# Row order instead of column pairs: the layout of the two middle products in a log-polar convolution kernel

## The chip, the cores and the metric

The kernel runs on one core of a Trainium2 chip. The metric is the device time of one execution in microseconds (us): 1636.28 us is the median of three runs before the change (1635.61 to 1636.46). Five engines work side by side and meet at semaphores: TensorE (PE in the profile) multiplies, VectorE (DVE) and ScalarE (ACT) prepare its inputs and take its results, GpSimd (POOL) and SyncE (SP) start transfers.

## The reference, cut to what matters

```python
def log_pooling(x):                      # x: 32 images, 256 channels, 28 x 28
    y = conv(x per channel, MASKS, pad 4)        # 12 fixed masks of 9 x 9, each an average of a bin
    ...                                          # laid out as 4 x 3 values for each pixel
xp = log_pooling(x)
out = conv(xp, w_conv1, stride (4, 3))           # 256 -> 256 channels, 12 values per pixel
out = out + conv(x, w_center, 1 x 1) + b_center
mean, var = over images and pixels, per channel
out = (out - mean) * rsqrt(var + EPS) * gamma + beta
return relu(out + x)
```

So each pixel gets 12 neighbourhood averages and itself, and a product with a 256 x 256 matrix for each. The six averages of the inner ring (next neighbours) are small sums of single pixels, the six of the outer ring are sums of larger boxes.

## The kernel before, in words

An image lies with its width W = 28 as the outer and its height H = 28 as the inner dimension: "column" u is a run of 28 values. A channel half (c = 0, 1; 128 partitions) of an image is one step s = 2 * image + c. The 256 output channels are two halves o = 0, 1. All inputs of TensorE are split into a high and a low part of fp32, and each product is three matmuls (hi*hi, lo weight*hi input, hi weight*lo input: the function `products`, lines 670 to 672).

The work on a pair of neighbouring image columns is shared: with U = 14 pairs, D1 = even + odd column and D2 = odd - even column are 14 columns of 28 = 392 values (HALF). Their products M1 and M2 (taps TAP_M1 and TAP_M2, three vertical shifts each) go into PSUM banks 4 to 7; the sum and the difference of M1 and M2 give the two columns of a pair of the output. This is "the middle": the inner-ring and centre taps that stand in one column.

In the kernel before, D1, D2, M1 and M2 are stored in STRIPES = 7 stripes of STRIPE = 56 values. A stripe holds two columns interleaved: value (h, k) with k the column in the stripe stands at 2 * h + k. A tap that is shifted by one row is therefore shifted by 2 values within every stripe, and covers SHORTER = 54 of its 56 values: a matmul over 7 runs of 54 with a pitch of 56.

For each image VectorE (one in-order queue) works through, for c = 0 and then c = 1:

1. four instructions that make the inner inputs: the differences `d03`, then D1, then D2 (392 values each, written in stripes), then the vertical sums VD (`v_ready`);
2. for c = 0, `take_middle` of the image before: M2 from PSUM and M1 from its copy `m1_copy` are added and subtracted into `y_stage`, one half o at a time;
3. when ScalarE has made the high parts (`split_inner`, line 370; it waits for `v_ready` and for `inner_done`, which TensorE sends after the inner products of the step before), the low part of the inner inputs;
4. the box sums, their pooled pairs and low parts (j = 0, 1, 2); for c = 0, behind the low part of j = 0, `take_y` of the image before, which adds banks 0 to 3 to `y_stage` and sends `y_ready`.

For each step TensorE (in order) does 36 matmuls of the middle, 24 of 392 columns for the other inner taps (behind `y_ready` for c = 0, since they start banks 0 to 3 anew), and 72 of 364 columns for the outer ring. After the last image a second phase loads y and x of all images again, scales, adds and stores them; it is bound by its transfers.

Of the kernel before, what the change touches and what calls it, by code (L numbers as in the profile page):

```python
# [7 lines left out]
def conv_bn_relu_program(nc, x, x_wide, w_raw, b_center, gamma, beta, out, y_dram):  # L8
# [7 lines left out]
    IMAGES, P, CH, W, H = x.shape  # L16
# [4 lines left out]
    HW = H * W  # L21
    U = W // 2
    HALF = U * H
# [4 lines left out]

    STRIPES, STRIPE = U // 2, 2 * H
    SHORTER = STRIPE - 2
    TALL = H + 2


# [27 lines left out]
    BANK = 512  # L64
    MBANK = 2 * CH

    ctx = ExitStack()
    with ctx:
# [6 lines left out]
        def view(buf, first, *dims):  # L75
            whole = buf[:, :]
            return bass.AP(whole.tensor, whole.offset + first, [list(whole.ap[0]), *map(list, dims)])

        start_of, end_of, used = {}, {}, [0]
        with ExitStack() as phase1:  # L80
# [16 lines left out]
            inner = reused("inner", 4 * HALF)  # L97
            pooled = reused("pooled", 2 * PAIR)
            INNER = 6 * HALF
            inner_split = reused("inner_split", 2 * INNER, F32R)  # L100
# [5 lines left out]
        y_stage = sb("y_stage", CH * HW)  # L106
        m1_copy = sb("m1_copy", CH * HALF)

        D1, D2, VD, SD = 0, HALF, 2 * HALF, 4 * HALF
# [55 lines left out]
        acc = ctx.enter_context(nc.psum_tensor("acc", [P, 8 * BANK], F32))  # L165
# [30 lines left out]
        middle_taken = sem("middle_taken")  # L196
# [250 lines left out]
        def _(dve):  # L447
            add = lambda out_, a, b: nc.vector.tensor_tensor(out_, a, b, ALU.add)  # L448
            sub = lambda out_, a, b: nc.vector.tensor_tensor(out_, a, b, ALU.subtract)  # L449
# [43 lines left out]
                        in1=view(hi, hi_at, (1, (b - a) * CHANNELS)).bitcast(F32),  # L493
                        op0=ALU.mult, op1=ALU.subtract).then_inc(w_lo_ready, 1)

            striped = (STRIPE, STRIPES), (1, 2), (2, H)
            every_other_column = (4 * H, STRIPES), (2 * H, 2), (1, H)

            def take_middle(image):

                dve.wait_ge(m1_copied, image + 1)
                wait_from_one(dve, y_saved, 16 * image)
                wait_from_one(dve, y_measured, MOMENTS * image)
                for o in range(CH):
                    m2 = view(acc, (MBANK + CH + o) * BANK, *striped)
                    m1 = view(m1_copy, o * HALF, *striped)
                    add(view(y_stage, o * HW, *every_other_column), m2, m1)
                    last = sub(view(y_stage, o * HW + H, *every_other_column), m1, m2)
                last.then_inc(middle_taken, 1)

            def take_y(image):
                dve.wait_ge(pooled_done, PAIRS * CH * (image + 1))
# [41 lines left out]
            def image_steps(image, first=False, second=False):  # L554
                for c in range(CH):
                    s = CH * image + c

                    def columns(first_column, step, n, *more):
                        return view(x_pad, c * X_PAD + (first_column + 2) * H, *more, (step * H, n), (1, H))

                    dve.wait_ge(x_loaded[c], 16 * (image + 1))
                    wait_from_one(dve, inner_lo_ready, 2 * s)
                    sub(view(d03, 1, (U * TALL, 2), (TALL, U), (1, H)),
                        columns(-1, 2, U, (H, 2)), columns(1, 2, U, (H, 2))).then_inc(d_ready, 1)
                    even, odd = (view(x_pad, c * X_PAD + (q + 2) * H, *every_other_column) for q in range(2))
                    add(view(inner, D1, *striped), even, odd)
                    sub(view(inner, D2, *striped), odd, even)
                    dve.wait_ge(d_ready, s + 1)
                    add(view(inner, VD, (HALF, 2), (H, U), (1, H)),
                        view(d03, 0, (U * TALL + 1, 2), (TALL, U), (1, H)),  # L570
                        view(d03, 1, (U * TALL + 1, 2), (TALL, U), (1, H))).then_inc(v_ready, 1)
                    if first:
                        lo_of_weights(c, range(INNER_GROUPS))
                    if c == 0 and not first:
                        take_middle(image - 1)

                    dve.wait_ge(inner_hi_ready, 2 * s + 1)
                    sub(view(inner_split, INNER, (1, SD)), view(inner, 0, (1, SD)),
                        view(inner_split, 0, (1, SD)).bitcast(F32)).then_inc(inner_lo_ready, 1)

                    dve.wait_ge(row2_ready, 16 * (s + 1))
                    add(view(row3, 1, (ROW3_H, W + 2), (1, H)), view(row2, 4, (ROW2_H, W + 2), (1, H)),
                        columns(0, 1, W + 2)).then_inc(row3_ready, 1)

                    dve.wait_ge(row3_ready, s + 1)
                    add(view(row3v, 2, (ROW3V_H, W + 2), (1, H + 1)), view(row3, 0, (ROW3_H, W + 2), (1, H + 1)),
                        view(row3, 1, (ROW3_H, W + 2), (1, H + 1))).then_inc(row3v_ready, 1)

                    dve.wait_ge(inner_hi_ready, 2 * s + 2)
                    sub(view(inner_split, INNER + SD, (HALF, 2), (H, U), (1, H)),  # L590
                        view(d03, 2, (U * TALL - 2, 2), (TALL, U), (1, H)),
                        view(inner_split, SD, (HALF, 2), (H, U), (1, H)).bitcast(F32)).then_inc(inner_lo_ready, 1)

                    if first:
                        lo_of_weights(c, range(FIRST_OUTER_GROUP - 1, len(GROUPS)))
                        if c == 0:
                            transform_weights(1)

                    dve.wait_ge(row3v_ready, s + 1)
                    add(view(box4, 0, (BOX4_H, W + 2), (1, H + 3)), view(row3v, 0, (ROW3V_H, W + 2), (1, H + 3)),  # L600
                        view(row3v, 2, (ROW3V_H, W + 2), (1, H + 3))).then_inc(box4_ready, 1)
                    add(view(box3, 1, (BOX3_H, W + 2), (1, H + 2)), view(row3v, 1, (ROW3V_H, W + 2), (1, H + 2)),
                        view(row3, 1, (ROW3_H, W + 2), (1, H + 2))).then_inc(box3_ready, 1)

                    dve.wait_ge(box4_ready, s + 1)
                    pooled_sums(s, c, 0, box4, 0, 4 * BOX4_H + 3, BOX4_H, row2, 0, 5 * ROW2_H + 8, ROW2_H)
                    dve.wait_ge(box3_ready, s + 1)
                    pooled_sums(s, c, 1, box3, 4, 4 * BOX3_H - 4, BOX3_H, row2, 8, 5 * ROW2_H - 8, ROW2_H)
                    lo_of_pooled(s, c, 0)
                    if c == 0 and not first:  # L610
                        take_y(image - 1)
                    dve.wait_ge(ends_ready, 16 * (s + 1))
                    short_sum(s, c, 0)
                    short_sum(s, c, 1).then_inc(pooled_ready, 1)
                    lo_of_pooled(s, c, 1)
                    lo_of_pooled(s, c, 2)
                    if second and c == 0:
                        make_pivot()
# [44 lines left out]
        def _(pe):  # L663
            def products(c, o, tap, place, buf, hi, lo, *dims, start=False, stop=False):

                hi_w, hi_at = w_part(c, 0, tap)
                lo_w, lo_at = w_part(c, 1, tap)
                hi_w, lo_w = (view(w, at + o * P, (1, P)) for w, at in ((hi_w, hi_at), (lo_w, lo_at)))
                hi_in, lo_in = view(buf, hi, *dims), view(buf, lo, *dims)
                nc.tensor.matmul(place, hi_w, hi_in, start=start, stop=False)  # L670
                nc.tensor.matmul(place, lo_w, hi_in, start=False, stop=False)  # L671
                return nc.tensor.matmul(place, hi_w, lo_in, start=False, stop=stop)  # L672
# [8 lines left out]
            with pe.Fori(0, IMAGES) as image:  # L681
                for c in range(CH):
# [5 lines left out]
                    for m, (tap, data) in enumerate(((TAP_M1, D1), (TAP_M2, D2))):  # L688
                        for o in range(CH):
                            bank = (MBANK + CH * m + o) * BANK  # L690
                            products(c, o, tap + 1, view(acc, bank, (1, HALF)),
                                     inner_split, data, INNER + data, (1, HALF), start=c == 0)

                            shorter = (STRIPE, STRIPES), (1, SHORTER)
                            products(c, o, tap, view(acc, bank + 2, *shorter),
                                     inner_split, data, INNER + data, *shorter)
                            last = products(c, o, tap + 2, view(acc, bank, *shorter),
                                            inner_split, data + 2, INNER + data + 2, *shorter, stop=c == CH - 1)
                    if c == CH - 1:
                        last.then_inc(m_done, 1)  # L700
                    pe.wait_ge(w_lo_ready, c * len(GROUPS) + INNER_GROUPS)
# [1 line left out]
                    for o in range(CH):  # L703
                        if c == 0:
                            pe.wait_ge(y_ready, CH * image + FREE)
                        for q, (with_v, with_d) in enumerate(((TAP_D, TAP_C), (TAP_A, TAP_F))):
# [4 lines left out]
                            last = products(c, o, with_d, place, inner_split, at, INNER + at, (1, HALF))  # L711
# [58 lines left out]
```

## Time and profile before

| what | value |
|---|---|
| median of three runs | 1636.28 us |
| the profiled execution's own time | 1636.42 us |
| its span, first to last instruction | 1634.7 us |
| PE busy | 1460.9 us (89%), 8468 matmuls |
| DVE busy | 1421.3 us (87%), 1391 instructions |
| ACT busy | 640.0 us (39%) |
| second phase (scale, add, store) | from about 1480 us on, with TensorE done |

Busy time is the union of an engine's instructions. A matmul's record overlaps the next one's, so its cost in a stream is read from the distance between starts, not from its duration. VectorE's records overlap by about 0.09 us in the same way. The granted clock is that of TensorE: 1.00 is 2.4 GHz, 0.50 is 1.2 GHz. "Idle before, releaser" is the time an engine stood still ahead of an instruction and what ended it.

### The profile page before, as it was taken

To read this page: it belongs to the slowest core of one execution; us is meant where nothing else is said; L and a number is where in the kernel's file an instruction comes from. 1 tells how busy PE (TensorE), PEld (TensorE's weight loads), DVE (VectorE), ACT (ScalarE), POOL (GpSimd) and SP (SyncE) were. 2 spreads that over 40 slices of the span, in tenths; PEclk is the share of its full clock that TensorE was granted. 3 is DMA by queue.
4 is the path that set the end of the run, shared out by engine and by line. 5 is a ranking of instruction groups with operands and counts; after the bars stand their busy time and mean duration, and the time that the engine had idled before them with its cause. 6 is when DMAs were issued, how large, how long until landed. Compare 5 with 4: busy or idle time off the path is not lost.

```text
span 1634.7 us, 22849 instructions
## 1 busy us (share of the span) xinstructions
PE 1460.9 (89%) x8468; PEld 1459.7 (89%) x8468; DVE 1421.3 (87%) x1391; ACT 640.0 (39%) x689; POOL 112.3 (7%) x144
## 2 busy tenths in 40 slices
PE   6999999999999999999999999999999999992000
PEld 6899999999999999999999999999999999992000
DVE  7999999999999999999999999999999999986323
ACT  3334434434334343433433334433343334335423
POOL 1000000000000000000000000000000000000000
PEclk8999999999999999999999999999999999996555
DMA  6455554555555555455554555545555555579999
GB/s 200 108 132 146 136 134 127 125 144 128 120 123 134 142 136 139 127 127 136 136 121 118 139 132 138 144 125 128 132 141 128 112 133 132 136 271 420 425 425 379
DMA packets 65479, 268.75 MB, mean 164 GB/s; under 512 B 7616, under 2 KB 7616, under 8 KB 65472
## 3 DMA queue, kind: packets, MB, share of 16 engines
q1 hardware_dynamic: 42176, 173.38, 31.4%
q0 software_dynamic: 18432, 69.61, 24.6%
q10 hardware_dynamic: 4864, 25.69, 3.8%
q8 instruction: 2, 0.03, 0.0%
q14 instruction: 5, 0.04, 0.0%
HBM read 218.07 MB, written 50.58 MB: 164 GB/s over the span
## 4 chain that ended last, share of the span: by engine, by line
PE 86%; SPq 5%; DMA 4%; DVE 3%; ACT 1%; issue 1%; ACTq 0%; DVEq 0%; POOLq 0%
PE acc L671 29%; PE acc L672 29%; PE acc L670 28%; SPq L311 4%; DMA phase<-x 2%; SPq L308 2%; DMA row<-x_wide 1%; DMA out<-phase 1%; DVE pooled L448 1%; DVE pooled_split L449 0%; ACT phase L440 0%; DVE inner_split L449 0%; ACT m_copy L396 0%; DVE y_stage L448 0%; DVE row3v L448 0%
## 5 line engine op out<-in xcount | busy, mean ns | idle before, releaser
L380 ACT ACTIVATE pooled_split<-pooled 128x1456 fp32r<-128x1456 f32 x192 | 273.5, 1425 | 609.5 <-DVE pooled L448 609.5
L449 DVE TENSOR_TENSOR pooled_split<-pooled,pooled_split 128x1456 fp32r<-128x1456 f32 x192 | 314.9, 1667 | 0.3 <-ACT pooled_split L380 0.3
L670 PE MATMUL acc<-pooled_split,w_first 128*128 128x364 f32 x768 | 252.7, 329 | 4.8 <-DVE pooled_split L449 4.8
L671 PE MATMUL acc<-pooled_split,w_first 128*128 128x364 f32 x768 | 253.6, 330 | 0.0
L672 PE MATMUL acc<-pooled_split,w_first 128*128 128x364 f32 x768 | 253.5, 330 | 0.0
L672 PE MATMUL acc<-pooled_split,w_outer 128*128 128x364 f32 x768 | 252.8, 329 | 0.0
L671 PE MATMUL acc<-pooled_split,w_outer 128*128 128x364 f32 x768 | 252.5, 329 | 0.0
L670 PE MATMUL acc<-pooled_split,w_outer 128*128 128x364 f32 x768 | 252.0, 328 | 0.0
L670 PE MATMUL acc<-inner_split,w_first 128*128 128x392 f32 (+1 forms) x640 | 219.5, 343 | 13.0 <-DVE inner_split L449 9.0
L672 PE MATMUL acc<-inner_split,w_first 128*128 128x392 f32 (+1 forms) x640 | 218.3, 341 | 0.0
L671 PE MATMUL acc<-inner_split,w_first 128*128 128x392 f32 (+1 forms) x640 | 218.1, 341 | 0.0
L671 PE MATMUL acc<-inner_split,w_inner 128*128 128x392 f32 (+1 forms) x640 | 218.0, 341 | 0.0
L672 PE MATMUL acc<-inner_split,w_inner 128*128 128x392 f32 (+1 forms) x640 | 217.5, 340 | 0.0
L670 PE MATMUL acc<-inner_split,w_inner 128*128 128x392 f32 (+1 forms) x640 | 217.2, 339 | 0.0
L448 DVE TENSOR_TENSOR pooled<-box,row 128x1456 f32<-128x1456 f32 x128 | 208.2, 1668 | 0.0
L449 DVE TENSOR_TENSOR inner_split<-inner,inner_split 128x1568 fp32r<-128x1568 f32 x64 | 114.6, 1791 | 95.7 <-ACT inner_split L370 95.7
L370 ACT ACTIVATE inner_split<-inner 128x1568 fp32r<-128x1568 f32 x64 | 96.9, 1514 | 188.7 <-PE acc L672 167.8
L670 PEld LDWEIGHTS acc<-pooled_split,w_first 128*128 128x128 f32 x768 | 145.0, 189 | 5.1 <-DVE pooled_split L449 5.1
L672 PEld LDWEIGHTS acc<-pooled_split,w_first 128*128 128x128 f32 x768 | 144.8, 189 | 0.0
L671 PEld LDWEIGHTS acc<-pooled_split,w_first 128*128 128x128 f32 x768 | 144.7, 188 | 0.0
L671 PEld LDWEIGHTS acc<-pooled_split,w_outer 128*128 128x128 f32 x768 | 144.5, 188 | 0.0
L672 PEld LDWEIGHTS acc<-pooled_split,w_outer 128*128 128x128 f32 x768 | 144.4, 188 | 0.0
(80 smaller groups left out, 2146.6 us busy)
## 6 DMA issues: line engine op xcount, KB each, us to landing
row<-x_wide SPq DMA_DIRECT2D x64, 558.0 KB, 3.7
row<-x_wide POOLq DMA_DIRECT2D x64, 558.0 KB, 7.3
ends<-x_wide SPq DMA_DIRECT2D x64, 504.0 KB, 3.9
ends<-x_wide POOLq DMA_DIRECT2D x64, 504.0 KB, 5.9
x_pad<-x SPq DMA_DIRECT2D x64, 392.0 KB, 3.1
y_dram<-y_stage SPq DMA_DIRECT2D x31, 784.0 KB, 8.5
phase<-y_dram SPq DMA_DIRECT2D x30, 784.0 KB, 29.2
phase<-x SPq DMA_DIRECT2D x30, 784.0 KB, 30.2
```

The costliest lines, as they stand in the source:

```text
L308: sp.dma_start(y_slot(d), y_dram[tail_image(round_, d)]).then_inc(tail_loaded[d], 16)
L311: sp.dma_start(x_slot_whole(d), x[tail_image(round_, d)].rearrange("p c w h -> p c (w h)"))\
L370: nc.scalar.activation(view(inner_split, 0, (1, SD)), view(inner, 0, (1, SD)), ACT.Copy)\
L380: nc.scalar.activation(view(pooled_split, 2 * j * PAIR, (1, PAIR)), view(pooled, (PAIRS * c + j) % 2 * PAIR, (1, PAIR)), ACT.Copy)\
L448: add = lambda out_, a, b: nc.vector.tensor_tensor(out_, a, b, ALU.add)
L449: sub = lambda out_, a, b: nc.vector.tensor_tensor(out_, a, b, ALU.subtract)
L670: nc.tensor.matmul(place, hi_w, hi_in, start=start, stop=False)
L671: nc.tensor.matmul(place, lo_w, hi_in, start=False, stop=False)
L672: return nc.tensor.matmul(place, hi_w, lo_in, start=False, stop=stop)
```

## The change

The interleaved stripes are replaced by whole rows: value (h, u) of D1, D2, M1 and M2 stands at 14 * h + u. A shift by one row is then a shift by 14 values in one run of 378 (HALF - U). On VectorE the two instructions that write D1 and D2 write neighbouring values 14 words (56 bytes) apart instead of 2 words (8 bytes), and `take_middle` reads M1 and M2 at that step. As both halves o now fit one access pattern, `take_middle` has two instructions of 784 values instead of four of 392.

```diff
-    STRIPES, STRIPE = U // 2, 2 * H
-    SHORTER = STRIPE - 2
+    SHORTER = HALF - U
...
-            striped = (STRIPE, STRIPES), (1, 2), (2, H)
-            every_other_column = (4 * H, STRIPES), (2 * H, 2), (1, H)
+            by_rows = (1, U), (U, H)
+            every_other_column = (2 * H, U), (1, H)
...
-                for o in range(CH):
-                    m2 = view(acc, (MBANK + CH + o) * BANK, *striped)
-                    m1 = view(m1_copy, o * HALF, *striped)
-                    add(view(y_stage, o * HW, *every_other_column), m2, m1)
-                    last = sub(view(y_stage, o * HW + H, *every_other_column), m1, m2)
-                last.then_inc(middle_taken, 1)
+                m2 = view(acc, (MBANK + CH) * BANK, (BANK, CH), *by_rows)
+                m1 = view(m1_copy, 0, (HALF, CH), *by_rows)
+                add(view(y_stage, 0, (HW, CH), *every_other_column), m2, m1)
+                sub(view(y_stage, H, (HW, CH), *every_other_column), m1, m2).then_inc(middle_taken, 1)
...
-                    add(view(inner, D1, *striped), even, odd)
-                    sub(view(inner, D2, *striped), odd, even)
+                    add(view(inner, D1, *by_rows), even, odd)
+                    sub(view(inner, D2, *by_rows), odd, even)
...
-                            shorter = (STRIPE, STRIPES), (1, SHORTER)
-                            products(c, o, tap, view(acc, bank + 2, *shorter),
-                                     inner_split, data, INNER + data, *shorter)
-                            last = products(c, o, tap + 2, view(acc, bank, *shorter),
-                                            inner_split, data + 2, INNER + data + 2, *shorter, stop=c == CH - 1)
+                            products(c, o, tap, view(acc, bank + U, (1, SHORTER)),
+                                     inner_split, data, INNER + data, (1, SHORTER))
+                            last = products(c, o, tap + 2, view(acc, bank, (1, SHORTER)),
+                                            inner_split, data + U, INNER + data + U, (1, SHORTER), stop=c == CH - 1)
```

VectorE's queue in the loop over images, c = 0, from the differences `d` to the low part of the inner inputs, before the change:

```order
L449 TENSOR_TENSOR d<-x_pad 128x28x28
L448 TENSOR_TENSOR inner<-x_pad 128x7x2x28
L449 TENSOR_TENSOR inner<-x_pad 128x7x2x28
L568 REGISTER_ALU
L448 TENSOR_TENSOR inner<-d 128x784
L220 ISA
L220 REGISTER_ALU
L448 TENSOR_TENSOR y_stage<-acc,m_copy 128x14x28
L449 TENSOR_TENSOR y_stage<-m_copy,acc 128x14x28
L448 TENSOR_TENSOR y_stage<-acc,m_copy 128x14x28
L449 TENSOR_TENSOR y_stage<-m_copy,acc 128x14x28
```

and in the same place after it:

```order
L447 TENSOR_TENSOR d<-x_pad 128x28x28
L446 TENSOR_TENSOR inner<-x_pad 128x14x28
L447 TENSOR_TENSOR inner<-x_pad 128x14x28
L564 REGISTER_ALU
L446 TENSOR_TENSOR inner<-d 128x784
L218 ISA
L218 REGISTER_ALU
L446 TENSOR_TENSOR y_stage<-acc,m_copy 128x28x28
L447 TENSOR_TENSOR y_stage<-m_copy,acc 128x28x28
```

Nothing is moved: the four instructions of `take_middle` become two of twice the size, and D1 and D2 (`inner<-x_pad`) keep their place. TensorE's queue keeps its 132 matmuls for each step in the same order; 24 of the 36 of the middle read 378 values in one run instead of 7 times 54.

## Rows read from the trace of the kernel before

**Rows 1.** Busy time by stretch (--windows): PE, PEld, DVE, ACT, POOL, clock, DMA share, GB/s.
```profile
100.00:1440.00 1340.00, 1340.00 (x7816) 1340.00 (x7815) 1242.48 (x1190) 528.13 (x560) 102.95 (x119) 1.00 0.54 131
1460.00:1500.00 40.00, 20.18 (x119) 19.88 (x117) 21.50 (x38) 14.86 (x21) 0.00 (x0) 0.78 1.01 419
1500.00:1634.00 134.00, 0.00 (x0) 0.00 (x0) 50.84 (x53) 50.79 (x55) 0.00 (x0) 0.50 0.99 413
```
**Rows 2.** VectorE's timeline, one image in the loop: start, us, instruction, idle before.
```profile
808.88 0.97 DVE L449 TENSOR_TENSOR d<-x_pad 128x784 f32<-128x784 f32 x1
...
813.47 1.79 DVE L449 TENSOR_TENSOR inner_split<-inner,inner_split 128x1568 fp32r<-128x1568 f32 x1 [1.78 <-ACT inner_split L370]
...
836.12 1.79 DVE L449 TENSOR_TENSOR inner_split<-inner,inner_split 128x1568 fp32r<-128x1568 f32 x1 [1.49 <-ACT inner_split L370]
...
849.33 1.73 DVE L448 TENSOR_TENSOR pooled<-box,ends 128x728 f32<-128x728 f32 x2
...
854.15 0.97 DVE L449 TENSOR_TENSOR d<-x_pad 128x784 f32<-128x784 f32 x1
```
**Rows 3.** PE's timeline: first matmul of each section of two steps.
```profile
801.02 0.34 PE L670 MATMUL acc<-inner_split,w_first 128*128 128x392 f32 x1
...
807.39 0.34 PE L670 MATMUL acc<-inner_split,w_first 128*128 128x392 f32 x1
...
811.67 0.33 PE L670 MATMUL acc<-pooled_split,w_first 128*128 128x364 f32 x1
...
823.64 0.34 PE L670 MATMUL acc<-inner_split,w_inner 128*128 128x392 f32 x1
...
830.04 0.34 PE L670 MATMUL acc<-inner_split,w_inner 128*128 128x392 f32 x1
```
**Rows 4.** Groups by line and form: the instructions that the change touches, and neighbours.
```profile
L448 DVE TENSOR_TENSOR inner<-d 128x784 f32<-128x784 f32 x64 | 62.0, 968 | 0.0
...
L449 DVE TENSOR_TENSOR inner<-x_pad 128x392 f32<-128x392 f32 x64 | 35.7, 558 | 0.0
L448 DVE TENSOR_TENSOR inner<-x_pad 128x392 f32<-128x392 f32 x64 | 35.7, 558 | 0.0
L448 DVE TENSOR_TENSOR y_stage<-acc,m_copy 128x392 f32<-128x392 f32 x64 | 35.6, 556 | 1.1 <-ACT m_copy L387 1.1
...
L448 DVE TENSOR_TENSOR pooled<-box,row 128x1456 f32<-128x1456 f32 x128 | 208.2, 1668 | 0.0
```
**Rows 5.** Groups by line and form: GpSimd's memsets, the only far-spaced writes.
```profile
L237 POOL MEMSET x_pad<- 128x56 f32 x2 | 0.3, 146 | 0.0
...
L237 POOL MEMSET box<- 128x30 f32 x2 | 0.2, 154 | 0.0
L237 POOL MEMSET x_pad<- 128x112 f32 x1 | 0.2, 193 | 0.0
...
L237 POOL MEMSET row<- 128x30 f32 x1 | 0.2, 157 | 0.0
```
**Rows 6.** VectorE's timeline, images 1 and 2, where it waits for no one else's pace.
```profile
63.53 0.97 DVE L449 TENSOR_TENSOR d<-x_pad 128x784 f32<-128x784 f32 x1
64.42 0.56 DVE L448 TENSOR_TENSOR inner<-x_pad 128x392 f32<-128x392 f32 x1
...
65.38 0.97 DVE L448 TENSOR_TENSOR inner<-d 128x784 f32<-128x784 f32 x1
66.26 0.56 DVE L448 TENSOR_TENSOR y_stage<-acc,m_copy 128x392 f32<-128x392 f32 x1
...
68.15 1.78 DVE L449 TENSOR_TENSOR inner_split<-inner,inner_split 128x1568 fp32r<-128x1568 f32 x1
...
79.58 1.84 DVE L448 TENSOR_TENSOR y_stage<-acc,y_stage 128x784 f32<-128x784 f32 x2
...
86.17 2.37 DVE L522 BATCH_NORM_STATS2 pivot_stats<-y_stage 128x6 f32<-128x392 f32 x4
...
89.14 0.98 DVE L449 TENSOR_TENSOR d<-x_pad 128x784 f32<-128x784 f32 x1
...
93.53 1.79 DVE L449 TENSOR_TENSOR inner_split<-inner,inner_split 128x1568 fp32r<-128x1568 f32 x1 [1.58 <-ACT inner_split L370]
...
110.00 0.97 DVE L449 TENSOR_TENSOR d<-x_pad 128x784 f32<-128x784 f32 x1
```
**Rows 7.** PE's timeline, its first inner matmul of image 1 and of image 31.
```profile
81.48 0.44 PE L670 MATMUL acc<-inner_split,w_first 128*128 128x392 f32 x1 [4.04 <-DVE y_stage L448]
...
1441.12 0.34 PE L670 MATMUL acc<-inner_split,w_first 128*128 128x392 f32 x1
```
**Rows 8.** Windows around the stall in image 1, columns as in group 1.
```profile
77.00:82.00 5.00, 0.96 (x6) 0.63 (x5) 5.00 (x5) 2.36 (x2) 0.00 (x0) 1.00 0.40 114
82.70:86.10 3.40, 3.40 (x12) 3.40 (x11) 3.40 (x3) 1.42 (x1) 0.78 (x1) 0.51 0.59 104
```

## The prediction

> **What bounds the kernel now.** I read the stretches first [rows 1]: between 100 and 1440 us TensorE is busy all the time at clock 1.00, VectorE 1242.48 of 1340 us, ScalarE 528.13. TensorE sets the pace, but VectorE is right behind it. From about 1480 us on TensorE is done and the transfers run at a share of 1.01 and 0.99: that second phase follows the first and nothing in it is changed.
>
> How far behind is VectorE? Its timeline of one image [rows 2] runs from 808.88 to 854.15, so an image takes 45.27 us, with two waits of 1.78 and 1.49 us, both for ScalarE's high parts, which in turn wait for TensorE's `inner_done`. That looks like 3.27 us of room, but not all of it is room. For c = 1 VectorE sends `v_ready` and at once needs the high part, so one ScalarE pass is a gap that stays however late VectorE is. Its own pace is seen in images 1 and 2, where it is not held by TensorE [rows 6]: the c = 0 step takes 63.53 to 86.17 = 22.64 us, the c = 1 step 89.14 to 110.00 = 20.86 us with that gap of 1.58 us in it. Together **43.50 us** of VectorE against 45.27 us of TensorE. The room is 1.77 us per image.
>
> Where it would hurt: `take_y` ends before the row at 849.33 [rows 2], and TensorE needs `y_ready` where its inner section of c = 0 starts, 807.39 + 45.27 = 852.66 [rows 3]: 3.3 us in hand, used up once and then gone. In image 1 TensorE does wait there, 4.04 us [rows 7].
>
> **TensorE's part.** From [rows 3]: 24 matmuls of 392 columns take 811.67 - 807.39 = 4.28 us, 178.3 ns each; 72 of 364 take 11.97 us, 166.25 ns each. On the line between them 378 columns cost 172.3 ns. The middle (12 of 392 and 24 of 378) takes 6.37 us for c = 0 and 830.04 - 823.64 = 6.40 us for c = 1; less 12 x 178.3 = 2.14 that is 4.25 us for 24, or 176.9 ns each. The seven short runs cost 4.6 ns over the line. I take it that one run loses all of that: 24 x 4.6 = 0.11 us per step, 0.22 us per image, so TensorE needs 45.05 us. If the excess is of another origin it stays 45.27.
> If TensorE still sets the pace this is worth 0.11 x 62 steps = 6.9 us, down to nothing.
>
> **VectorE's part.** The instructions of 784 and 1456 values take 968 and 1668 ns [rows 4]: 1.042 ns per value and 151 ns. By that 392 values take 559 ns, and D1 and D2, whose written neighbours are 8 bytes apart, take 558; `take_middle`, which reads both sources at 8 bytes, takes 556. So a step of two words is free. A step of 14 words stands in no row of VectorE. Call the extra time per value x ns.
> - Merging four instructions to two: they take 68.15 - 66.26 = 1.89 us now [rows 6]; instructions of 784 take up 0.89 and 0.88 us of the queue (63.53 to 64.42, 65.38 to 66.26), so two of them 1.77 us. A gain of 0.12 us per image.
> - D1 and D2: 2 x 392 values per step, 1568 per image. `take_middle`: 2 x 784 = 1568 per image. Together 3136 values, 3.136x us per image.
>
> VectorE's own pace becomes 43.50 - 0.12 + 3.136x = 43.38 + 3.136x us.
>
> **The size of x.** From below: 0, if the engine's memory port is indifferent to the step, as it is between 1 and 2 words. From above: 3.1, if a value on its own cost as much as four in a row. Two rows stand between. At a step of two words a pair shares what 16 bytes it touches, and the pair takes 2.08 ns; if each value now needs that slot for itself, x = 1.04. The only writes to far places in the trace are GpSimd's memsets [rows 5]: 56 contiguous values take 146 ns and 112 take 193, 0.84 ns each and 99 fixed, so 30 contiguous ones would take 124 ns; 30 values one per row of `box` and `row` take 154 and 157. That is 1.0 to 1.1 ns more for each value. Both point to the same number and I take **x = 1.0** for writes and reads.
> The Trainium skill speaks against this change here: SBUF — State Buffer, in its section Specifications (TRN2), says that SBUF has 16-byte lines and that full bandwidth wants two hits in each; this trace agrees as far as it goes (558 ns at a step of two words), and has no longer step. Vector Engine (DVE) Microarchitecture Reference, 5.2 Measured stream behaviour on trn2, lists 1.71 to 1.76 ns per value for steps to other regions on one port or two, and 2.50 for a step of 24 words, against 1.054 contiguous; by it x would be 0.66 to 1.46 and the time 1645 to 1723 us, an estimate from that page.
>
> **The sum.** With x = 1.0 VectorE's pace is 46.52 us per image, 1.47 more than TensorE needs: VectorE becomes the bound and TensorE waits at `y_ready` once per image. I count from wait to wait. `take_y` of image 1 ends at 79.58 + 1.84 = 81.42 [rows 6] (TensorE starts at 81.48 [rows 7]). Up to there VectorE works without a gap from the step s = 1 on; that stretch holds D1 and D2 of two steps and one `take_middle`, so it is late by 3.136x - 0.12 = 3.02 us: 84.44. (What step 0 loses goes into its wait for a transfer, and that wait is over 2 us.) Then 30 images at 46.52 = 1395.6 and the pivot statistics once, 89.14 - 86.17 = 2.97: **1483.0 us** for TensorE's first inner matmul of image 31. Before, it is at 1441.12 [rows 7]. What follows, 1636.42 - 1441.12 = 195.3 us of the profiled execution's own time (1.7 us of it outside the span), is TensorE's rest of the image and the transfers. VectorE keeps ahead there as now: after `take_y` it needs some 5 us for j = 1 and 2 of that step, TensorE reaches them after 4.28 + 4 us. So 1483.0 + 195.3 = 1678.3. The profiled execution lies 0.14 us above the median, which I drop: **1678 us**, 2.6% more. In general it is 1581.0 + 97.2x us, as long as this is over TensorE's own 1629.5. They meet at x = 0.50, and the time before is passed at x = 0.57.
>
> **Rivals.**
> - *The step is free or cheap* (x under 0.5), or only one side pays: with x = 1 on D1 and D2 alone, or on the reads alone (one source is PSUM), it is 1581.0 + 48.6 = 1629.6. TensorE stays the bound and the time is **1629.5 us**, faster. For: every row of VectorE is free of step costs. Against: GpSimd's rows, and that no such row goes past 8 bytes. The point is x = 0.57. Chance 0.14.
> - *Both cancel*: x between 0.53 and 0.60, within 3.3 us of before: 1633 to 1640. Chance 0.04.
> - *The price is higher* (x about 1.5): 1581.0 + 145.8 = **1727 us**. For: two streams of `take_middle` step at once, and the step is not a multiple of 16 bytes. Chance of over 1700: 0.27.
> - *The clock falls too.* After the stall of 4.04 us in image 1 the clock is 0.51 for 3.4 us [rows 8], which costs TensorE some 1.7 us. If each wait of 1.5 us did this, TensorE would need 45.05 + 1.7 = 46.75 us, 0.23 more than VectorE, some 7 us: **1685 us**. Chance 0.05; in the other cases such a fall would be hidden in the wait.
>
> **How the numbers follow.** My forecast, VectorE as bound with x between 0.6 and 1.25, has 0.50, and x = 1.0 stands for it; its own range is 1640 to 1703. The chance of slower by over 0.2% (3.3 us, what measurements of this kernel can tell from no change) is 0.50 + 0.27 + 0.05 = 0.82, within it 0.04, faster 0.14. The range leaves out the fast side below 1640 and what lies above x = 1.5: 1640 to 1727 us.
>
> **What the profile after would show.** D1 and D2 at 0.95 us instead of 0.558; `take_middle` as two instructions of 1.75 us each instead of 0.97; TensorE with an idle time of some 1.5 us per image ended by `y_stage`, some 45 us in all; ScalarE's `split_inner` waiting for `inner` rather than for TensorE; VectorE's waits for ScalarE only at c = 1, about 1.6 us; the middle section at 6.27 us instead of 6.38. The sum is wrong if D1 and D2 stay below 0.76 us and `take_middle` below 1.37 us each (x = 0.5), or if they and the reads differ: then each side counts 48.6 us per ns.

## The result: slower by 0.7%, with VectorE as the bound, at two thirds of the assumed price per value

The changed kernel takes 1648.36 us (median of four runs, 1647.85 to 1649.01) against 1636.37 us: ratio 1.0073, 95% interval 1.0061 to 1.0086. That is 12.0 us slower; the forecast was 1678 us, 41.7 us slower, in a range of 1640 to 1727. So the direction was right and the size was not. Its profiled execution took 1648.46 us.

The busy time by stretch of the changed kernel, columns as in [rows 1]:

```profile
100.00:1440.00 1340.00, 1334.45 (x7773) 1325.41 (x7772) 1289.06 (x1121) 521.60 (x557) 101.88 (x118) 1.00 0.54 131
```

TensorE did 7773 matmuls here in the time of 7816 and was idle for 5.55 us; VectorE is busy for 46.6 us more. The clock is 1.00 as before. The groups of the changed instructions, which answer to [rows 4]:

```profile
L447 DVE TENSOR_TENSOR inner<-x_pad 128x392 f32<-128x392 f32 x64 | 56.1, 876 | 0.0
...
L446 DVE TENSOR_TENSOR inner<-x_pad 128x392 f32<-128x392 f32 x64 | 55.1, 861 | 0.0
...
L446 DVE TENSOR_TENSOR y_stage<-acc,m_copy 128x784 f32<-128x784 f32 x32 | 50.2, 1570 | 0.0
L447 DVE TENSOR_TENSOR y_stage<-m_copy,acc 128x784 f32<-128x784 f32 x32 | 49.9, 1560 | 0.0
```

D1 and D2 take 861 and 876 ns instead of 558, `take_middle` 1570 and 1560 ns instead of the 968 of a contiguous instruction of its size. The waits, in total, times and longest:

```profile
ACT inner_split L368 <- DVE inner L446: 221.5, 64, 4.9
...
DVE inner_split L447 <- ACT inner_split L368: 48.9, 31, 1.6
...
PEld acc L666 <- DVE y_stage L446: 20.2, 31, 5.2
```

ScalarE's `split_inner` waits all 64 times for VectorE's sums and never for TensorE (before: 56 times for TensorE). VectorE waits only 31 times, once per image, with the pass of ScalarE that it can't hide. And once per image TensorE's weight loads wait for `y_stage`, the `take_y` that the prediction named. VectorE's timeline of one image, which answers to [rows 2] and [rows 6]:

```profile
703.43 0.97 DVE L447 TENSOR_TENSOR d<-x_pad 128x784 f32<-128x784 f32 x1
704.32 0.87 DVE L446 TENSOR_TENSOR inner<-x_pad 128x392 f32<-128x392 f32 x1
705.02 0.88 DVE L447 TENSOR_TENSOR inner<-x_pad 128x392 f32<-128x392 f32 x1
705.73 0.97 DVE L446 TENSOR_TENSOR inner<-d 128x784 f32<-128x784 f32 x1
706.63 1.57 DVE L446 TENSOR_TENSOR y_stage<-acc,m_copy 128x784 f32<-128x784 f32 x1
708.10 1.57 DVE L447 TENSOR_TENSOR y_stage<-m_copy,acc 128x784 f32<-128x784 f32 x1
709.59 1.78 DVE L447 TENSOR_TENSOR inner_split<-inner,inner_split 128x1568 fp32r<-128x1568 f32 x1
...
732.44 1.79 DVE L447 TENSOR_TENSOR inner_split<-inner,inner_split 128x1568 fp32r<-128x1568 f32 x1 [1.58 <-ACT inner_split L368]
...
748.90 0.97 DVE L447 TENSOR_TENSOR d<-x_pad 128x784 f32<-128x784 f32 x1
```

The image takes 748.90 - 703.43 = 45.47 us, with no idle time but the one gap of 1.58 us. From start to start D1 and D2 take 0.705 us of the queue each (704.32 to 705.73) instead of 0.475: 4 x 0.23 = 0.92 us per image, or x = 0.59 ns per value (x is the prediction's extra time for a value at the far step). `take_middle` takes 2.96 us (706.63 to 709.59) instead of 1.89. 43.50 + 0.92 + 1.07 = 45.49: the pace is the sum of its parts. Taken from the pace alone, x is (45.47 - 43.38) / 3.136 = 0.67 ns over writes and reads together.

What TensorE waits for, at the start of its inner section of c = 0:

```profile
813.22 0.34 PE L667 MATMUL acc<-inner_split,w_first 128*128 128x378 f32 x1
813.39 0.33 PE L668 MATMUL acc<-inner_split,w_first 128*128 128x378 f32 x1
813.86 0.45 PE L666 MATMUL acc<-inner_split,w_first 128*128 128x392 f32 x1
814.14 0.34 PE L667 MATMUL acc<-inner_split,w_first 128*128 128x392 f32 x1
```

From 813.39 to 814.14 there are 0.75 us for two matmuls that otherwise take 0.35: 0.4 us lost per image, so TensorE alone would need 45.47 - 0.40 = 45.07 us. A matmul's drawn duration hides most of this gap; it is seen in the starts.

### The profile page after: what moved, and what is told of

The parts are those of the page before. It is cut to its first block, busy times and chain, and to the rows that moved or that the text cites. A ratio compares the mean times of both kernels' runs of the same rounds, so it can differ in the third digit from the quotient of the medians.

```text
span 1646.8 us, 22785 instructions
## 1 busy us (share of the span) xinstructions
PE 1461.5 (89%) x8468; PEld 1450.3 (88%) x8468; DVE 1482.4 (90%) x1327; ACT 636.8 (39%) x689; POOL 112.1 (7%) x144
## 4 chain that ended last, share of the span: by engine, by line
DVE 54%; issue 29%; SPq 6%; ACT 4%; DMA 4%; PE 2%; DVEq 1%; ACTq 0%; POOLq 0%
DVE pooled L446 12%; DVE pooled_split L447 9%; DVE inner_split L447 7%; DVE y_stage L446 5%; DVE box L446 4%; SPq L309 4%; DVE row L446 4%; DVE d L447 4%; DVE inner L446 4%; DVE inner L447 3%; ACT inner_split L368 3%; DMA phase<-x 2%; SPq L306 2%; DMA row<-x_wide 1%; PE acc L666 1%
## 5 line engine op out<-in xcount | busy, mean ns | idle before, releaser
L666 PEld LDWEIGHTS acc<-inner_split,w_first 128*128 128x128 f32 x640 | 121.3, 190 | 32.5 <-DVE y_stage L446 20.2
L666 PEld LDWEIGHTS acc<-pooled_split,w_outer 128*128 128x128 f32 x768 | 144.2, 188 | 0.4 <-DVE pooled_split L447 0.4
```

## The experiments

All times are medians unless said otherwise, each beside runs of the kernel before on the same chip (1636.4 to 1636.7 us).

**1. TensorE alone by rows.** VectorE keeps its stripes, so the middle's values are not the reference's.

```diff
 # the kernel before, with SHORTER = HALF - U, and (not shown: the inputs and the third tap likewise)
-                            shorter = (STRIPE, STRIPES), (1, SHORTER)
-                            products(c, o, tap, view(acc, bank + 2, *shorter), ...
+                            products(c, o, tap, view(acc, bank + U, (1, SHORTER)), ...
```

> TensorE's matmuls of the middle read and write one run of 378; VectorE still writes and reads stripes, so the middle's values are not the reference's. Theory A (VectorE's far steps alone cost the time): VectorE's pace stays 43.50 us per image, TensorE's falls by 0.22 us to 45.05, the time by up to 6.9 us, about 1629.5 us. Rival B (the new layout hurts on TensorE's side, for instance by its offset of 14 words, and the slow VectorE is only what is seen): 1636 us or more. Rival C (the 378-column matmuls gain nothing): 1636 us.

1630.98 us, ratio 0.9967 (0.9955 to 0.9980). The half of the change that is on TensorE is a gain, of 5.4 us.

**2. VectorE alone by rows.** TensorE keeps its 7 runs of 54.

```diff
 # the changed kernel, and (not shown: the inputs and the third tap likewise)
-                            products(c, o, tap, view(acc, bank + U, (1, SHORTER)), ...
+                            shorter = (2 * H, U // 2), (1, 2 * H - 2)
+                            products(c, o, tap, view(acc, bank + 2, *shorter), ...
```

> VectorE writes D1 and D2 and reads M1 and M2 by rows, in two instructions; TensorE still works on 7 runs of 54, so the middle's values are not the reference's. Theory A: VectorE sets the pace with 45.47 us per image as in the changed kernel, the same 1648 us within 1 us, although TensorE is 0.22 us per image slower. Rival B: the loss was in TensorE's part, about 1636 us.

1649.14 us, ratio 1.0080 (1.0064 to 1.0097): the whole loss. Without TensorE's gain of 5.4 us the time is only 0.8 us longer than the changed kernel's (1649.14 against 1648.36), which the two intervals can't tell from nothing. The effects of the two halves do not add up; the slower engine's pace is the time.

**3 and 4. Half of VectorE's part.** First D1 and D2 alone at the far step (`take_middle` reads stripes), then `take_middle` alone.

```diff
 # 3: the changed kernel, and in take_middle
+                for o in range(CH):
+                    m2 = view(acc, (MBANK + CH + o) * BANK, *striped)
+                    m1 = view(m1_copy, o * HALF, *striped)
...
 # 4: the changed kernel, and
-                    add(view(inner, D1, *by_rows), even, odd)
-                    sub(view(inner, D2, *by_rows), odd, even)
+                    add(view(inner, D1, *striped), even, odd)
+                    sub(view(inner, D2, *striped), odd, even)
```

> D1 and D2 are written by rows and TensorE works by rows; VectorE still reads M1 and M2 in stripes with four instructions, so the output is not the reference's. Theory A (two paces, the larger one counts): D1 and D2 cost 0.93 us per image more, VectorE needs 43.50 + 0.93 = 44.43 us, less than TensorE's 45.05, so 1629.5 us, faster than before. Rival D (each extra us on VectorE costs its share, for instance through a chain that runs over both engines): about half of the loss stays, 1640 us or more.

> M1 and M2 are read by rows in two instructions and TensorE works by rows; D1 and D2 are still written in stripes, so the output is not the reference's. Theory A: VectorE needs 43.50 + 1.07 = 44.57 us per image, less than TensorE's 45.05, so 1629.5 us. Rival D: 1642 us or so.

1632.35 us (ratio 0.9976, 0.9967 to 0.9986) and 1633.15 us (0.9980, 0.9970 to 0.9989). Either half of the cost disappears, and the kernel is faster than before; only both together pass TensorE. That is two paces with the larger one counting, and not a share of the loss for each microsecond. Both are 1.4 to 2.2 us above experiment 1. TensorE's first inner matmul of image 1 answers to the first of [rows 7] and stands at 81.48 before and at 81.60 in experiment 1; in experiments 3 and 4:

```profile
82.44 0.70 PE L670 MATMUL acc<-inner_split,w_first 128*128 128x392 f32 x1 [4.06 <-DVE y_stage L446]
```
```profile
82.64 0.69 PE L668 MATMUL acc<-inner_split,w_first 128*128 128x392 f32 x1 [4.87 <-DVE y_stage L446]
```

In image 1 TensorE waits for VectorE in every one of these kernels, so there VectorE's extra time counts: 0.84 and 1.04 us more than in experiment 1. What is left of the 1.4 and 2.2 us is not taken apart.

**5. The price of a step, operand by operand.** Ahead of the changed kernel's work, VectorE adds and ScalarE copies 784 values with one operand, or two, at a step of k words, k = 1, 2, 4, 7, 14, 28, 56, each instruction waiting for the one before.

```diff
+            chained(nc.vector.tensor_tensor(view(m1_copy, 0, (HALF, 2), (1, 14), (14, HALF // 14)),
+                view(box4, 0, (HALF, 2), (1, HALF)), view(box3, 0, (HALF, 2), (1, HALF)), ALU.add))
...
+            chained(nc.vector.tensor_tensor(view(m1_copy, 0, (2, 7), (14, 28), (1, 2)),
+                view(box4, 0, (1, HALF)), view(box3, 0, (1, HALF)), ALU.add))
...
```

Of the two lines shown, the first steps the output by 14 words and the second writes adjacent pairs that hop by 14 words. The left-out lines put `box4`, then `box4` and `box3`, then the PSUM tile `acc`, then `acc` and `box3` at the step.

> The changed kernel with instructions ahead of its work that write or read 784 fp32 values at steps of 1, 2, 4, 7, 14, 28 and 56 words, one operand at a time: VectorE's output in SBUF, one SBUF source, both, a PSUM source, PSUM and SBUF both; and the same on ScalarE's PSUM source and SBUF output. Contiguous ones take 968 ns. Theory A1 (two neighbours within 16 bytes are needed, then a fixed price): steps 1 and 2 at 968 ns, all of 4 and more at about 1430 ns written (x = 0.59) and 1570 ns read. Theory A2 (the price depends on the step): 14 differs from 28 and 56. For the reads, A3: the price is SBUF's alone and the PSUM source is free at 968 ns; A4: both pay, 1570 ns each. Pairs of neighbours that hop by 14 words should cost nothing (559 ns for 392).

VectorE's timeline of the probe. Lines 663 to 669 step the output, k = 1 to 56; 674 is one SBUF source and 681 both at k = 14; 684 to 690 are a PSUM source; 695 is PSUM and SBUF at k = 14; 698 and 699 are pairs that hop by 14 words, written and read:

```profile
5.95 0.98 DVE L663 TENSOR_TENSOR m_copy<-box 128x784 f32<-128x784 f32 x1
6.96 0.98 DVE L664 TENSOR_TENSOR m_copy<-box 128x784 f32<-128x784 f32 x1
7.97 1.55 DVE L665 TENSOR_TENSOR m_copy<-box 128x784 f32<-128x784 f32 x1
9.56 1.56 DVE L666 TENSOR_TENSOR m_copy<-box 128x784 f32<-128x784 f32 x1
11.15 1.50 DVE L667 TENSOR_TENSOR m_copy<-box 128x784 f32<-128x784 f32 x1
12.69 1.60 DVE L668 TENSOR_TENSOR m_copy<-box 128x784 f32<-128x784 f32 x1
14.32 1.63 DVE L669 TENSOR_TENSOR m_copy<-box 128x784 f32<-128x784 f32 x1
...
21.18 1.50 DVE L674 TENSOR_TENSOR m_copy<-box 128x784 f32<-128x784 f32 x1
...
31.19 1.50 DVE L681 TENSOR_TENSOR m_copy<-box 128x784 f32<-128x784 f32 x1
...
40.07 0.97 DVE L688 TENSOR_TENSOR m_copy<-acc,box 128x784 f32<-128x784 f32 x1
...
48.26 1.49 DVE L695 TENSOR_TENSOR m_copy<-acc,box 128x784 f32<-128x784 f32 x1
...
53.05 0.57 DVE L698 TENSOR_TENSOR m_copy<-box 128x392 f32<-128x392 f32 x1
53.65 0.57 DVE L699 TENSOR_TENSOR m_copy<-box 128x392 f32<-128x392 f32 x1
```

Steps of 1 and 2 words are free; 4 to 56 cost 0.52 to 0.66 us per 784 values, so x is 0.66 to 0.84 ns, and 0.67 at 14. One SBUF operand or two, written or read: the same. The PSUM source is free at every k (0.97 us in all seven), and so are pairs (0.57 us for 392 values). Each of these instructions ran once. ScalarE: PSUM source at any step 0.82 us, SBUF output at 4 words and more 1.50 to 1.63 us.

ScalarE's output at k = 1, 2, 4 and 14:

```profile
60.35 0.82 ACT L440 ACTIVATE m_copy<-acc 128x784 f32<-128x784 f32 x1
61.21 0.86 ACT L442 ACTIVATE m_copy<-acc 128x784 f32<-128x784 f32 x1
62.10 1.54 ACT L444 ACTIVATE m_copy<-acc 128x784 f32<-128x784 f32 x1
...
65.27 1.50 ACT L448 ACTIVATE m_copy<-acc 128x784 f32<-128x784 f32 x1
```

So A1 holds for where the price starts and nearly for its size (1.50 us at 14 words, written or read, where 1.43 and 1.57 were expected). A2 holds in small: 14 words cost 0.10 to 0.13 us less than 28 and 56. A3 holds for the reads: what `take_middle` pays is its SBUF source M1. The probe does not show why the loop has 0.59 ns for writes and 0.76 for reads; its price of 0.67 is that of both together.

**6. A version that beats both.** If PSUM is free at any step, whoever reads PSUM should do the turning. ScalarE's copy of M1 reads by rows and writes columns, and VectorE reads only M2 at the step.

```diff
 # the changed kernel, and
-                nc.scalar.activation(..., view(acc, MBANK * BANK, (BANK, CH), (1, HALF)), ACT.Copy)
+                nc.scalar.activation(..., view(acc, MBANK * BANK, (BANK, CH), (1, U), (U, H)), ACT.Copy)
...
-                m1 = view(m1_copy, 0, (HALF, CH), *by_rows)
+                m1 = view(m1_copy, 0, (HALF, CH), (1, HALF))
```

> The changed kernel, but ScalarE's copy of M1 puts it into columns (it reads PSUM at a step of 14 words and writes one run), so take_middle reads only M2 (PSUM) at the far step and M1 as one run. The output is the reference's. If the PSUM source is free at that step (A3), VectorE's pace falls to 43.38 + 0.93 = 44.31 us and TensorE sets the pace: 1629.5 us, faster than both kernels. If it costs the same as both together (A4), VectorE stays at 45.47 us: 1648 us. ScalarE's copy should grow from 0.81 us to some 0.8 to 1.3 us, without effect on the time.

1632.34 us, ratio 0.9975 (0.9965 to 0.9984), 16 us below the changed kernel. Its groups:

```profile
L446 DVE TENSOR_TENSOR y_stage<-acc,m_copy 128x784 f32<-128x784 f32 x32 | 31.0, 969 | 0.6 <-ACT m_copy L385 0.6
L447 DVE TENSOR_TENSOR y_stage<-m_copy,acc 128x784 f32<-128x784 f32 x32 | 31.0, 968 | 0.0
...
L385 ACT ACTIVATE m_copy<-acc 128x784 f32<-128x784 f32 x32 | 26.4, 824 | 42.4 <-PE acc L668 42.4
```

`take_middle` is at the contiguous price again, and ScalarE's copy costs the 0.82 us that it did. The edit is one access pattern in the copy and its counterpart in `take_middle`. The time is 2.8 us over the 1629.5 expected; that difference is not taken apart.

**7 and 8. VectorE's room, measured.** The kernel before, with D1 and D2 issued once and twice more into a spare tile that nothing reads. A version that computed D1 and D2 twice in place, with the same load and the same forecast as experiment 7, gave no time.

```diff
 # 7: the kernel before, and (not shown: in 8 the added pair stands twice, with a wait between)
                     sub(view(inner, D2, *striped), odd, even)
+                    add(view(spare, 0, *striped), even, odd)
+                    sub(view(spare, HALF, *striped), odd, even)
```

> The kernel before, with the instructions of D1 and D2 issued once more into a spare tile that nothing reads: four more instructions of 392 values per image, 4 x 0.475 = 1.90 us on VectorE. Theory A (two paces, the larger one counts): VectorE's pace is 43.50 + 1.90 = 45.40 us against TensorE's 45.27, so nearly all of it goes into the room of 1.77 us. By the count from wait to wait TensorE's first inner matmul of image 31 comes at 81.42 + 1.90 + 30 x 45.40 + 2.97 = 1448.3 us, so 1643.6 us. Rival D (all of VectorE's time counts): 1.90 x 31 = 59 us more, 1695 us.

> The kernel before, with D1 and D2 issued twice more into a spare tile (with one semaphore wait between the two pairs, about 0.15 us): some 2 x (4 x 0.475 + 0.15) = 4.1 us per image on VectorE. Theory A: VectorE's pace is 47.6 us, 2.3 over TensorE's; 81.42 + 4.1 + 30 x 47.6 + 2.97 = 1516.5, so 1712 us. Together with the run of two spare instructions this gives the slope: from 1.90 to 4.1 us per image every us counts 31 times (68 us), while from 0 to 1.90 it counts only 7 us. Rival D: 4.1 x 31 = 127 us more than before, 1763 us.

1645.60 us (ratio 1.0055, 1.0038 to 1.0072) and 1713.22 us (1.0468, 1.0450 to 1.0485). The first 1.90 us per image cost 9 us in all, the next 2.2 us cost 67.6. If all of VectorE's added time counted, it would be 59 and 127 us; so the room of 1.77 us and the count from wait to wait hold for a load of known size. VectorE's `take_y` in two images of the second of them:

```profile
704.89 1.84 DVE L450 TENSOR_TENSOR y_stage<-acc,y_stage 128x784 f32<-128x784 f32 x2
...
752.45 1.85 DVE L450 TENSOR_TENSOR y_stage<-acc,y_stage 128x784 f32<-128x784 f32 x2
```

47.56 us per image, 47.6 expected.

**9 and 10. Which side of the matmul the short runs cost.** The version of experiment 6, with the shifted taps' input, or their output, in 7 runs of 54.

```diff
 # 9: input in stripes                          # 10: output in stripes (not shown: the third tap likewise)
+   view(acc, bank + U, (1, SHORTER)),          view(acc, bank + 2, *shorter),
+   inner_split, data, INNER + data, *shorter   inner_split, data, INNER + data, (1, SHORTER)
```

> The kernel with M1 turned by ScalarE, where TensorE sets the pace, but the shifted taps read their input in 7 runs of 54 with a pitch of 56 and write PSUM in one run of 378; the middle's values are not the reference's. If the 4.6 ns per matmul came from the input side, a matmul of 378 columns is back at some 177.2 ns (one run: 172.7) and the image at 45.3 us; if from the output side, 172.7 ns and 45.08 us. I expect the input side: with broken runs of 26 in PSUM (the pooled pair j = 2) nothing was lost.

> The same kernel with the input of the shifted taps in one run of 378 and PSUM written in 7 runs of 54 with a pitch of 56; the middle's values are not the reference's. Input side to blame: 172.7 ns per matmul of 378 columns. Output side: 177.2 ns.

The first matmul of the middle and of the section behind it, input in stripes:

```profile
802.77 0.34 PE L666 MATMUL acc<-inner_split,w_first 128*128 128x392 f32 x1
...
809.14 0.34 PE L666 MATMUL acc<-inner_split,w_first 128*128 128x392 f32 x1
```

and output in stripes:

```profile
799.90 0.34 PE L666 MATMUL acc<-inner_split,w_first 128*128 128x392 f32 x1
...
806.19 0.35 PE L666 MATMUL acc<-inner_split,w_first 128*128 128x392 f32 x1
```

The middle takes 6.37 us, the value of before in [rows 3], against 6.29, the value of the version of experiment 6. The whole gain of one run comes from the input in SBUF; these broken output runs in PSUM cost nothing. The times are 1637.64 and 1632.46 us, one run each, so the reading rests on the matmuls' starts.

## Why the prediction was right or wrong

- **What bounds it, and the room.** Right. VectorE at 43.50 us per image against 45.27, a gap of one ScalarE pass that can't be used, `take_y` as the place of the wait: all as in the trace after, and the loads of experiments 7 and 8 came out at 1645.6 and 1713.2 where the same count gave 1643.6 and 1712.
- **TensorE's part.** Right in kind and nearly in size: 0.11 us per step forecast, and 0.08 us (6.37 to 6.29) in the middle of experiment 10. TensorE's pace in experiment 1 is 45.08 us per image, forecast 45.05. Its worth where TensorE is the bound was put at 6.9 us; experiment 1 gave 5.4.
- **Merging four instructions to two.** Right in size: in experiment 6 the two take 968 ns, as counted.
- **The size of x.** This is the step that failed: "Both point to the same number and I take x = 1.0 for writes and reads". In the loop it was 0.59 for the writes, and for the reads (2.96 - 1.77) / 1.568 = 0.76; over both it was 0.67. That two sources agreed on 1.0 was chance. GpSimd's memsets priced another engine's stores. The pair's slot of 2.08 ns is not the price of a value on its own, which is 1.04 + 0.67 = 1.71 ns.

  What the prediction gave as an estimate from the Trainium skill, Vector Engine (DVE) Microarchitecture Reference, 5.2 Measured stream behaviour on trn2, was nearer at its lower end: 1.71 to 1.76 ns per value is x = 0.66 to 0.71, and the probe measured 0.67 at 14 words. The 2.50 ns that the same section of the Trainium skill gives for a step of 24 words appears at none of the steps run here (28 words: 1.60 us for 784 values); 24 itself was not run. The rule in that section of the Trainium skill that full rate needs adjacent pairs is contradicted at a step of 2 words, which is free (0.98 us written, 0.97 read). The Trainium skill's 16-byte line with two hits (SBUF — State Buffer, Specifications (TRN2)) fits all seven steps and the pairs. The Trainium skill's statement (PSUM — Partial Sum Buffer, Specifications (TRN2)) that any non-contiguous pattern in PSUM slows matmuls significantly is not borne out by experiment 10: 6.29 us with 7 runs of 54.
- **The sum.** With the measured prices the wait-to-wait count gives 1385.7 + 48.6 x (0.59 + 0.76) = 1451.3 us for TensorE's first inner matmul of image 31; it came at 1450.45. The steps around x were sound, and 97.2 us per ns of x turned an error of 0.33 ns into 32 us. The time fell inside the stated range because that range was wide: x = 0.67 lies near the lower end of the forecast's own 0.6 to 1.25.
- **"What follows ... 195.3 us" stays.** Off by 2.7: it is 1648.46 - 1450.45 = 198.0. SyncE's queue, in the kernel before and then after, shows why:

```profile
1439.93 0.43 SPq L301 DMA_DIRECT2D y_dram<-y_stage  x1
1448.41 0.33 SPq L308 DMA_DIRECT2D phase<-y_dram  x1
```
```profile
1452.46 0.43 SPq L299 DMA_DIRECT2D y_dram<-y_stage  x1
1460.81 0.33 SPq L306 DMA_DIRECT2D phase<-y_dram  x1
```

The last y is stored when `take_y` is done: 1.2 us before TensorE's inner section in the kernel before, 2.0 us after it now, since VectorE's lead of 3.3 us is gone. The first load of the second phase waits for that store (8.0 us before, 7.8 us after) and comes 3.1 us later against TensorE, and that phase runs at the transfers' rate. The other kernels bear this out: the same stretch is 197.3 to 198.0 us in experiments 2, 7 and 8, where VectorE leads, and 194.6 to 195.6 us in 1, 3, 4, 6, 9 and 10, where TensorE does. No run changes the store alone.
- **Rivals.** "Only one side pays" did not come, since D1, D2 and M1 all pay; experiments 3 and 4 made it, and it is faster, as that rival had it (1629.6 forecast, 1632.4 and 1633.2 measured). It named PSUM as a source that might not pay, and that source does not. "The price is higher" failed: at 14 words a PSUM source and an SBUF source together take 1.49 us, no more than one SBUF source (1.50). "Both cancel" needed x up to 0.60. A fall of the clock in the loop did not come: it is 1.00 from 100 to 1440 us. Nor does it in experiment 8, where TensorE stands still for 2.2 us in every image: 0.99 there.

## What to carry to other kernels

Where an engine has only 4% of room per iteration behind the bound, a layout that helps the bound and costs that engine must be priced on that engine first. Two engines' costs are not added; the larger pace counts, and an edit may be free alone and expensive with a second one. Of a wait inside the loop, count as room only what shrinks when the engine falls behind. If a layout must be turned, turn it where PSUM is read, and keep successive SBUF values of one instruction at most 8 bytes apart or in adjacent pairs; 16 bytes and more cost time here, and 12 were not run.

## What the runs showed of the hardware

- VectorE in SBUF, fp32: a step of 1 or 2 words (8 bytes) is free, 4 words (16 bytes) and more, up to 56, cost 0.66 to 0.84 ns per value. The price depends little on the step, and not on read or write or on one or two operands; adjacent pairs that hop by 14 words pay nothing (0.57 us for 392 values). ScalarE's output in SBUF behaves alike: 0.82 and 0.86 us for 784 values at 1 and 2 words, 1.50 to 1.63 us from 4 words on. Its SBUF source was not run.
- A PSUM source at any step up to 56 words costs nothing on VectorE (0.97 us for 784 values) or ScalarE (0.82 us).
- TensorE reads 7 runs of 54 in SBUF nearly as slowly as one of 392 (176.9 and 178.3 ns from [rows 3]), though they hold 378 columns; in one run these take (6.29 - 2.14) / 24 = 172.9 ns. So a run of 54 seems to cost as much as 56 columns. That lengths that are no multiple of four values are rounded up is a guess from these numbers, with no run of its own.
- Not every break costs: in the kernel before, the pooled products with 13 input runs of 28 (j = 0 and 1) and those with one input run and 14 output runs of 26 (j = 2) take the same 3.99 us for 24 matmuls (starts at 811.67, 815.66, 819.65 and 823.64). Broken output runs in PSUM are free at 26 (there) and at 54 (experiment 10).
